# The first two batches of an attention and mixture-of-experts kernel put in another order

## The reference

```python
def xattn(q, k, v, mask, gamma, beta):          # k = v = ctx (8, 77, 256)
    logits = einsum('bsd,btd->bst', q, k) / sqrt(256)
    attn = softmax(where(mask == 0, -9e15, logits))
    x = einsum('bst,btd->bsd', attn, v)
    return layernorm(x) * gamma + beta
def ffn(x, w_gate, w_gate_up, w_down):          # E = 8 experts, F = 1024
    probs = softmax(x @ w_gate)                 # the two largest, renormalised
    g, u = split(einsum('bsd,edh->ebsh', x, w_gate_up))
    return sum over e of probs[e] * ((silu(g) * u) @ w_down[e])
x = x + xattn(layernorm(x), ctx, ctx, mask, gamma, beta)
x = x + ffn(layernorm(x), w_gate, w_gate_up, w_down)
```

## Time and profile before

| | |
|---|---|
| time, median of 3 runs | 436.49 us (436.16 to 436.55) |
| profiled execution, its own time | 436.5 us |
| span of its trace | 434.8 us |
| TensorE busy | 424.1 us, 98% |
| VectorE busy | 304.3 us, 70% |
| ScalarE busy | 216.3 us, 50% |
| GpSimd busy | 195.7 us, 45% |
| DMA | 44.17 MB, mean 102 GB/s |

### The profile page before, as it was taken

The page is one execution under the profiler, slowest core; times in us unless marked ns, Lnnn a source line. Parts: engine busy times, 40 slices in busy tenths (PEclk is TensorE's granted clock), DMA queues, the critical chain, the costliest instruction groups (busy, mean ns, idle before and its releaser), DMA issues.

```text
span 434.8 us, 10143 instructions
## 1 busy us (share of the span) xinstructions
PE 424.1 (98%) x2356; PEld 351.8 (81%) x2356; DVE 304.3 (70%) x749; ACT 216.3 (50%) x461; POOL 195.7 (45%) x217
## 2 busy tenths in 40 slices
PE   9999889999999999999999999999999999999995
PEld 5798457888888888888888888888888888888885
DVE  3878988885886478868856568858785567865633
ACT  3796636554563366365443356536634346434431
POOL 5463253554563434544543455544554444444312
PEclk9999999999999999999999999999999999999999
DMA  7785514452454125425531115442542225112212
GB/s 208 215 258 149 212 42 153 129 167 75 121 135 134 26 73 145 148 31 129 158 98 26 25 26 134 142 114 73 153 140 34 36 65 136 26 25 28 37 13 26
DMA packets 28621, 44.17 MB, mean 102 GB/s; under 512 B 2833, under 2 KB 22219, under 8 KB 28587
## 3 DMA queue, kind: packets, MB, share of 16 engines
q1 hardware_dynamic: 20358, 32.96, 23.8%
q0 software_dynamic: 7520, 10.41, 14.1%
q10 hardware_dynamic: 709, 0.32, 0.3%
HBM read 34.04 MB, written 9.65 MB: 100 GB/s over the span
## 4 chain that ended last, share of the span: by engine, by line
PE 92%; DVE 3%; ACT 2%; DMA 1%; issue 1%; POOL 0%; DVEq 0%; POOLq 0%
PE bank L1440 48%; PE bank L1463 16%; PE bank L1465 8%; PE bank L1453 8%; PE bank L1238 3%; PE bank L1424 2%; PE bank L1284 1%; PE bank L1307 1%; PE bank L1317 1%; PE bank L1270 1%; DMA tok<-rows_d,gather_i 1%; PE bank L1510 1%; ACT ctxT L1109 1%; DVE x_sb L702 1%; PE bank L1529 0%
## 5 line engine op out<-in xcount | busy, mean ns | idle before, releaser
L1440 PE MATMUL bank<-w,tokT_hi 128*128 (+1 forms) x616 | 170.0, 398 | 1.2 <-DVE tokT_lo L920 0.9
L1160 ACT ACTIVATE gated<-bank,row_rstd 128x512 f32<-128x512 f32 x77 | 53.0, 688 | 173.8 <-PE bank L1440 173.8
L1440 PEld LDWEIGHTS bank<-w,tokT_hi 128*128 128x128 f32 x616 | 110.0, 188 | 22.9 <-DVE tokT_lo L920 1.2
L1463 PE MATMUL bank<-w,aT_hi 128*128 (+1 forms) x304 | 116.4, 417 | 0.1
L929 DVE SCALAR_TENSOR_TENSOR act<-bank,row_rstd,gated 128x512 f32<-128x512 f32 x77 | 57.6, 749 | 78.3 <-ACT gated L1160 78.3
L588 POOL DMA_INDIRECT out<-y_sb,out_i x39 | 62.1, 1592 | 89.0 <-DVE y_sb L950 85.6
L1440 PE MATMUL bank<-w,tokT_lo 128*128 (+1 forms) x308 | 95.3, 390 | 0.0
L1465 PE MATMUL bank<-w,aT_lo 128*128 (+1 forms) x304 | 85.3, 281 | 0.0
L575 POOL TENSOR_TENSOR tok<-tok,beta_b 128x256 f32<-128x256 f32 x36 | 26.3, 730 | 97.3 <-DMA tok<-rows_d,gather_i 97.3
L1440 PEld LDWEIGHTS bank<-w,tokT_lo 128*128 128x128 f32 x308 | 57.8, 188 | 12.9
L1463 PEld LDWEIGHTS bank<-w,aT_hi 128*128 128x128 f32 x304 | 57.2, 188 | 10.4 <-DVE w L402 0.4
(11 more groups left out here) (190 smaller groups left out, 413.8 us busy)
## 6 DMA issues: line engine op xcount, KB each, us to landing
raw<-in_L_ffn_w_gate_up SPq DMA_DIRECT2D x32, 512.0 KB, 3.7
raw<-in_L_ffn_w_down SPq DMA_DIRECT2D x16, 512.0 KB, 3.7
rows_d<-x_sb SPq DMA_DIRECT2D x8, 265.0 KB, 4.7
x_sb<-in_x SPq DMA_DIRECT2D x8, 256.0 KB, 7.6
out<-x_sb SPq DMA_DIRECT2D x8, 256.0 KB, 4.7
out<-y_sb,out_i POOLq DMA_INDIRECT x39
tok<-rows_d,gather_i POOLq DMA_INDIRECT x38, 3.7
cap<-in_mask_BxSxS_ik SPq DMA_DIRECT2D x1, 462.0 KB, 6.3
```

Of the source, the lines that this page charges most:

```text
L1160: act_e.activation(gated[:, h, :], ps_g[h][:, :], ACT.Silu, scale=row_rstd[:, s:s + 1]).then_inc(gated_set, 1)
L1440: ins = pe.matmul(ps[:, :], tokens_[:, s, k, :], w.rearrange("p a g d -> p (a g) d"), start=(k == 0 and tokens_ is tokT_hi and part == 0), ...
L1463: pe.matmul(ps_y[:, :], aT_hi[:, h, c, :], w.rearrange("p a t d -> p (a t d)"), start=(h == 0 and c == 0), stop=False, skip_group_check=True)
```

## The change

The prologue grows from the first batch's scores to a written order of the first two batches, and the loop starts at i = 2. On TensorE x of batch 1 is turned ahead of logits(0), logits(0) and logits(1) stand in a row, and values(0) and values_gamma(0) come ahead of the second context (`turn_ctx(1)`). Most fillers of the front are gone. VectorE takes x_stats(0) while it waits for the column sums, bans(1) goes ahead of ctx_means(2), and x1(0) goes ahead of x_stats(4). `STATS` takes batch 3 alone, and then pairs 4, 5 and 6, 7. ScalarE centres batches 2 and 3 between exps(0) and exps(1), and batches 4 to 7 in iteration 2. GpSimd makes values_gamma(0) ahead of x_rstd(1). The splits of the weights stand an iteration later: split_high(0) to (2) at i = 3 to 5 and (3) at 7, split_low(0) and (1) at 4 and 5.

```diff
@@ -64,9 +64,9 @@
     REGION = FULL * P
     VAL = D + 1
     EPS_COL = 16.0 * EPS ** 0.5
-    CTX_AT = {0: 1, 2: 2, 3: 3}
+    CTX_AT = {1: 1, 2: 2, 3: 3}
     GROUPS = [range(0, 6), range(6, 12), range(12, 16)]
-    STATS = [range(0, 1), range(1, 2), range(2, 3), range(3, 5), range(5, 7), range(7, 8)]
+    STATS = [range(0, 1), range(1, 2), range(2, 3), range(3, 4), range(4, 6), range(6, 8)]
     assert PIECES % RAW == 0 and NBLK % 2 == 1 and HALF == 512 and TPB == 2 and KD == 2 and F == PIECE and D == 2 * P and D == 16 ** 2
     assert E * FULL == P and TOK <= 2048 and NT == 16
 
@@ -549,13 +549,17 @@
             pool.wait_ge(centred_set, 1)
             pool.tensor_copy(ctxT[:, :, :, T:TE], wg_sb[:, :, 0, :].unsqueeze(1).to_broadcast([P, B, KD, GC])).then_inc(ctxw_set, 1)
             x_rstd(0)
+            values_gamma(0)
             x_rstd(1)
-            values_gamma(0)
-            for i in range(B + 1):
+            x_rstd(2)
+            values_gamma(1)
+            scales(0)
+            x_rstd(3)
+            values_gamma(2)
+            for i in range(2, B + 1):
                 if i + 2 < len(STATS):
                     x_rstd(i + 2)
-                if i >= 1:
-                    scales(i - 1)
+                scales(i - 1)
                 if i + 1 < B:
                     values_gamma(i + 1)
 
@@ -838,11 +842,10 @@
                 step(tables, dve.tensor_copy(expert_t[:], expert_f[:]))
 
             ctx_means(0, 0, 2)
+            x_stats(0)
             dve.wait_ge(colsum_ps, 1)
             dve.scalar_tensor_tensor(out=wg_sb[:, :, 0, 0:E], in0=ps_colsum.unsqueeze(1).to_broadcast([P, KD, E]), scalar=-1.0 / D,
                                      in1=w_gate_sb[:], op0=ALU.mult, op1=ALU.add).then_inc(centred_set, 1)
-            bans(0, 0, 2)
-            x_stats(0)
             dve.wait_ge(centred_set, 1)
             dve.wait_ge(cols_ps, 1)
             dve.wait_ge(mean_col_set, 1)
@@ -850,25 +853,29 @@
                                      in1=ps_cols[:, 0:KD].unsqueeze(2).to_broadcast([P, KD, GC]), op0=ALU.mult, op1=ALU.mult).then_inc(wg_set, 1)
             dve.tensor_tensor(wg_sb[:, :, 2, :], wg_sb[:, :, 0, :], ps_cols[:, KD:2 * KD].unsqueeze(2).to_broadcast([P, KD, GC]),
                               ALU.mult).then_inc(wg_set, 1)
+            bans(0, 0, 2)
             dve.wait_ge(bias_ps, 1)
             dve.tensor_copy(bias_g[:], ps_bias).then_inc(bias_set, 1)
+            x_stats(1)
             masked_logits(0)
-            x_stats(1)
             ctx_means(1, 2, 4)
-            for i in range(B + 1):
+            masked_logits(1)
+            x_stats(2)
+            bans(1, 2, B)
+            ctx_means(2, 4, B)
+            x_stats(3)
+            masked_logits(2)
+            x1(0)
+            for i in range(2, B + 1):
                 if i + 2 < len(STATS):
                     x_stats(i + 2)
-                if i == 3:
+                if i == 4:
                     split_low(dve, 0)
-                if i == 4:
+                if i == 5:
                     split_low(dve, 1)
                 if i + 1 < B:
                     masked_logits(i + 1)
-                if i == 0:
-                    ctx_means(2, 4, B)
-                    bans(1, 2, B)
-                if i >= 1:
-                    x1(i - 1)
+                x1(i - 1)
                 if i == 4:
                     dve.wait_ge(const, 15)
                     choose(GROUPS[0])
@@ -1113,28 +1120,40 @@
             copy_xT(0)
             copy_ctxT(0)
             copy_xT(1)
-            for i in range(B + 1):
-                if i >= 1:
+            exps(0)
+            copy_xT(2)
+            copy_pT(0)
+            copy_ctxg(0)
+            centre(2)
+            centre(3)
+            exps(1)
+            copy_ctxT(1)
+            square(0)
+            square(1)
+            copy_pT(1)
+            copy_xT(3)
+            for i in range(2, B + 1):
+                if i > 2:
                     copy_pT(i - 1)
                 if i < B:
                     exps(i)
                 if i - 1 in CTX_AT:
                     copy_ctxg(CTX_AT[i - 1])
-                if i >= 1:
-                    square(TPB * (i - 1))
-                    square(TPB * (i - 1) + 1)
+                if i == 2:
+                    centre(4)
+                    centre(5)
+                square(TPB * (i - 1))
+                square(TPB * (i - 1) + 1)
                 if i + 2 < B:
                     copy_xT(i + 2)
-                if i < 3:
-                    centre(2 * i + 2)
-                    centre(2 * i + 3)
+                if i == 2:
+                    centre(6)
+                    centre(7)
                 if i in CTX_AT:
                     copy_ctxT(CTX_AT[i])
-                if i == 0:
-                    copy_ctxg(0)
-                if 2 <= i < 5:
-                    split_high(act_e, i - 2)
-                if i == 6:
+                if 3 <= i < 6:
+                    split_high(act_e, i - 3)
+                if i == 7:
                     split_high(act_e, 3)
             numbers(0, GROUPS[0])
             numbers(1, GROUPS[1])
@@ -1264,7 +1283,6 @@
                 pe.wait_ge(x_in[b], 16)
                 if b >= 1:
                     pe.wait_ge(xT_set, b)
-                    spin(1 if b < 4 else 0, bank[0])
                 for j in range(TPB):
                     for k in range(KD):
                         ins = pe.transpose(ps_xT[:, KD * j + k, :], x_sb[:, TPB * b + j, k * P:(k + 1) * P], ident[:])
@@ -1278,7 +1296,7 @@
                 pe.wait_ge(ban_set, min(b // 2, 1) + 1)
                 if b >= 2:
                     pe.wait_ge(pT_set, b - 1)
-                    spin(2 if b == 2 else 1, bank[2 + b % 2])
+                    spin(min(b - 2, 1), bank[2 + b % 2])
                 for j in range(TPB):
                     for k in range(KD):
                         pe.matmul(ps_logit[b % 2][:, j, :], xT[:, b % 2, KD * j + k, :], ctxT[:, b, k, :],
@@ -1354,40 +1372,44 @@
             for k in range(KD):
                 ins = pe.matmul(ps_colsum, ones_f[:], w_gate_sb[:, k, :], start=(k == 0), stop=(k == KD - 1))
             ins.then_inc(colsum_ps, 1)
-            spin(2, bank[3])
             turn_ctx(0)
-            spin(1, bank[3])
             pe.wait_ge(cols_in, 32)
             pe.transpose(ps_cols, cols_row[:], ident[0:2 * KD, 0:2 * KD]).then_inc(cols_ps, 1)
-            spin(4, bank[3])
-            pe.wait_ge(const, 5)
-            logits(0)
-            spin(1, bank[3])
+            spin(2, bank[3])
             pe.wait_ge(wg_set, 2)
             for k in range(KD):
                 ins = pe.matmul(ps_bias, ones_f[:], wg_sb[:, k, 2, :], start=(k == 0), stop=(k == KD - 1))
             ins.then_inc(bias_ps, 1)
+            spin(1, bank[3])
             turn_x(1)
-            spin(6, bank[3])
-            for i in range(B + 1):
+            pe.wait_ge(const, 5)
+            logits(0)
+            logits(1)
+            turn_x(2)
+            turn_probs(0)
+            gate_ctx(0)
+            values(0)
+            values_gamma(0)
+            turn_ctx(1)
+            turn_x(3)
+            turn_probs(1)
+            logits(2)
+            gate_ctx(1)
+            for i in range(2, B + 1):
                 if i + 2 < B:
                     turn_x(i + 2)
                 if i >= 7:
                     spin(2, bank[0])
-                if i >= 1:
-                    values(i - 1)
+                values(i - 1)
                 if i == B:
                     ranks(1, GROUPS[1])
                 if i + 1 < B:
                     logits(i + 1)
                 if i in CTX_AT:
                     turn_ctx(CTX_AT[i])
-                if i >= 1:
-                    values_gamma(i - 1)
+                values_gamma(i - 1)
                 if i < B:
                     turn_probs(i)
-                if i == 0:
-                    gate_ctx(0)
                 if i in CTX_AT:
                     gate_ctx(CTX_AT[i])
                 if i == 5:
```

## The result

The changed kernel takes 433.27 us (median of 7 executions, the lowest 431.67), the kernel before 436.16 beside it: ratio 0.9924, 95% interval 0.9909 to 0.994, some 3.3 us faster. The forecast was 433.8 with 432.8 to 435.7. In 2 of the 7, and in 3 of 12 when it was run again, it took 441 to 453 us: TensorE ran at half rate (1.2 GHz in place of 2.4) for a part of the front (one of the five has a trace that shows it, the other four a mean granted clock of 0.958 to 0.98); the ratios here leave such executions out, and of 54 executions of the kernel before none was above 439.33 us. I call it a fall when TensorE loses the full rate near 20 us, and a late rise when it stays at half rate from the start for tens of microseconds.

The account below looks back on a forecast made before the run. The front's chain was taken to be set by VectorE's wait for the third context, then ScalarE's iteration 2 up to gate_ctx(2): 24.38 - 21.7 = 2.7 us earlier, carried to the end, 436.5 - 2.7 = 433.8; range 432.8 to 435.7.

Parts of the forecast that it names:

- VectorE's wait for the third context: Front, ahead of ctx_means(2): VectorE arrives 1.4 us before the context of batches 4 to 7 lands at 14.4.
- ScalarE's steps of i = 2: From exps(2) at 17.5 through copies, centres and squares to copy_ctxT(2): 4.05 us, ending near 21.5, ahead of gate_ctx(2).
- the covered places: Loop and routing: copy_pT(3) covered by 0.3 us; values(7) 0.3 late at no cost; x1(4) nothing, at most 0.3.
- the tail that shifts as a whole: Behind x1(5): everything hangs on what lies ahead, so 2.7 us earlier there means 2.7 at the end.
- masked_logits(1) would not wait for the rstd: VectorE's front: gamma_b lands at 9.4, so x_rstd(1) ends near 10.8 and costs nothing; at 12.6 the gain is 1.4.
- the 24.38 of the chain: TensorE: taken as gate_ctx(2)'s place in the kernel before; less 21.7 after, it gave the 2.7 us gain.
- The rival that I called (1): Front: TensorE work alone counts and all waits are hidden; values(1) 3.6 us earlier, so 432.9 us; chance 0.07.
- a late rise as covered: Front: a clock rise late by 1 us costs half a us of TensorE time, covered by logits(2) being 1.4 early.
- a fall as excluded: TensorE's new waits of 0.6 and 1.0 us were held no longer than a gap that left the clock at 1.00.
- a row with 0.14 us of work in one microsecond: Windows row from 49 to 50 us: TensorE busy 0.14 of 1 us, granted clock 1.00; used against a fall.
- rival (4): Slower: clock falls in the gap before gate_ctx(2) for two batches, 8.7 us of work doubles, 442.5 us; chance 0.05.
- the wait of 1.0: TensorE ahead of gate_ctx(2), from 20.6 to 21.6 us, waiting for ScalarE's context copy.

Follow-up runs that it names:

- e1: Changed kernel with x_stats(3) ahead of ctx_means(2) on VectorE; 432.45 us, ratio 0.9906 to the kernel before.
- e2: Changed kernel with the third context's load issued behind x of batches 4 and 5; 5 of 6 executions took 442 to 454 us, the other 433.5.
- e5: Changed kernel with the weight splits back at their old iterations; 438.46 us, ratio 0.9922 to the kernel before without the long executions.
- e7: Changed kernel with copy_ctxT(2) ahead of centre(6) and centre(7) on ScalarE in iteration 2; 433.5 us, ratio 0.9909 to the kernel before.
- e13: e11 with the two fillers ahead of turn_ctx(0) put back; 432.23 us, ratio 0.9909 to the kernel before, none of 6 executions above 440.
- e14: e11 run again, word for word; 432.44 us, ratio 0.9909 to the kernel before, 2 of 6 executions above 440.
- e0: The changed kernel itself measured once more; 433.91 us over 12 executions, ratio 0.9942 to the kernel before.
- e12: Changed kernel with only the two fillers ahead of turn_ctx(0) put back; 433.15 us, ratio 0.9929 to the kernel before, 2 of 6 executions above 440.
- e4: Changed kernel with the 16 fillers put back, so the new order alone; 435.19 us, ratio 0.9989 to the kernel before.
- e9: Changed kernel with one filler ahead of values(0) and three ahead of gate_ctx(2); 434.27 us, ratio 0.9948 to the kernel before.
- e11: Changed kernel with third context loaded before the second mask, ctx_means(2) before bans(1), copy_ctxT(2) before centre(6) and centre(7), one filler before values(0); 431.91 us, ratio 0.9901.
- e3: Kernel before with the 16 fillers taken out and nothing moved; ratio 0.9966 to the kernel before, 4 of 9 executions took 442 to 444 us.

## Why the prediction was right, and where it was not

**The place and the mechanism were right.** VectorE's wait for the third context (1.4 us forecast, 1.35 measured), the path from there through ctx_means(2), masked_logits(2), exps(2) and ScalarE's steps of i = 2 to gate_ctx(2), the covered places (copy_pT(3), values(7), x1(4)) and the tail that shifts as a whole all stand in the trace. e1, e2, e5, e7 and e13 moved links (the load's landing, VectorE's order, ScalarE's order), and the links behind them followed as far as the rate held; e2's one execution at full rate is the measurement that doesn't bear it out. That masked_logits(1) would not wait for the rstd held as well: gamma_b was there at 8.4, a microsecond earlier than I took.

**The size was 0.4 us short, in three small terms.** I had exps(2) at 17.5, the end of the copy at 21.5 and gate_ctx(2) at 21.7; they came at 17.15, 21.04 and 21.09. Of these 0.6 us, 0.26 is the load, which landed at 14.2; 0.15 is ScalarE's steps (4.05 forecast, 3.9 measured), 0.15 the step from the copy to gate_ctx(2) (0.2 forecast, 0.05 measured), and the rest rounding. Against it stands a row read wrongly: the 24.38 of the chain is not where gate_ctx(2) starts. Before's timeline of TensorE has its first instruction at 24.21:

```profile
24.21 0.66 PE L1259 MATMUL bank<-wg_sb,ctxT 128*77 128x9 f32 x8
```

So my own walk gave 2.5 us and not 2.7, and 3.1 arrived, at gate_ctx(2) as at x1(5).

**The rival that I called (1) was wrong in its reason.** VectorE's wait is there in after's trace. TensorE's own work counts only once that wait is gone: the traces of e13 and e14 reach gate_ctx(2) with no gap and are 3.6 and 4.1 us ahead of before at x1(5), where after is 3.1 ahead.

**The step that failed is the clock.** I took a late rise as covered, and a fall as excluded by a row with 0.14 us of work in one microsecond, and gave the rival 0.05. Of 19 executions, 4 have the mean clock of a fall and 1 had a late rise (e0's trace). The price of a fall was of the size of rival (4) in three of the four: 442.5 worked out, 441.6, 443.7 and 443.5 measured; the fourth took 450.8. A late rise, which I had costed for one microsecond only, took 452.5. The median doesn't show it, since most executions kept the full rate. Three things were missing. The gap in that row is 0.86 us at most, which is shorter than the wait of 1.0 that I held against it. The landing of the load is not a constant: the traces have it from 13.4 to 15.3 us (e12, e5), and a late one widens TensorE's gaps (0.58 us in after, 1.30 and 0.67 in e5, landing 1.09 later). And a single quiet row shows that one gap did not bring a fall in one execution, not that such a gap never does. No trace of after itself shows a fall; that it falls behind TensorE's gaps at that place is taken from e1 and e7.

## What to carry to other kernels

When filler work is taken out, walk each engine's order to the next thing with a time of its own, here a load: it sets how much of the gain arrives, and it is the next thing to move (traces of e13 and e14). Fillers that look like waste may hold TensorE's rate; look at the spread of many executions, not only at one profile, before taking them out. Putting back the few that stand ahead of the rise, and closing the wait, left no long execution here, though in six only (e13). And change fillers and order together or compare both halves: here either half alone gave 0.1 to 0.3%, and both 0.6 to 0.8%.

## What the runs showed of the hardware

- The moment at which TensorE's rate rises differs between executions, even though up to the column sums (the first 6 us) TensorE's instructions are the same in all: durations turn to the short ones before 5 us in e4, near 5.5 in e9, near 7 in before, near 10.4 in e11, near 28 in e3, and near 52 in e0.
- Once lost in this front, the full rate did not come back for 17 to 41 us though TensorE had hardly a gap: from 21 or 22 us to near 39 in e1, near 42 in e7, near 57 in e5, near 62 in e2.
- The granted clock of the windows view reads 1.00 in e0 and e3 where durations are those of half rate.
- The same load, issued at the same time, landed at 14.4 (before), 14.2 (after), 15.0 (e7), 15.3 (e5) and 13.4 us (e12).
